# Last stage of a transformer layer on one Trainium2 core: the token sums move from VectorE to TensorE, the residual's shift to ScalarE, the scaled add to VectorE

## What is computed

```
x = x + layernorm(attention(layernorm(x)))
x = x + layernorm(ffn(layernorm(x)))
ffn(x) = y + z
y: mixture of 16 experts (128 -> 176 -> 128), each token goes to its best 2, weighted
z: shared expert (128 -> 352 -> 128)
layernorm(v) = (v - mean(v)) / sqrt(var(v) + 1e-5), over the 128 channels
```

## Time and profile before

| | before |
|---|---|
| median of 3 runs | 1185.89 us (1185.29 to 1187.51) |
| profiled execution: its own time | 1186.67 us |
| profiled execution: span of its profile | 1184.1 us |
| TensorE busy | 1055.4 us, 89% of the span |
| VectorE (DVE) busy | 845.6 us, 71% |
| ScalarE (ACT) busy | 738.9 us, 62% |
| GpSimd (POOL) busy | 846.1 us, 71% |

### The profile page before, as it was taken

One profiled execution on the slowest core, in us unless ns is written; L12 is line 12 of the kernel. 1 busy time (PEld: TensorE's weight loads), 2 busy tenths in 40 slices (PEclk: granted clock), 3 DMA queues, 4 the chain that ended last, 5 costly groups with the idle time before them and its releaser, 6 DMA issues.

```text
span 1184.1 us, 26787 instructions
## 1 busy us (share of the span) xinstructions
PE 1055.4 (89%) x8458; PEld 687.7 (58%) x8458; DVE 845.6 (71%) x2285; ACT 738.9 (62%) x1617; POOL 846.1 (71%) x984
## 2 busy tenths in 40 slices
PE   4589999999999999999999999999768999999700
PEld 2346555666656666566666665654336888888500
DVE  4587888778787787877878778774234666666586
ACT  1137778677776776867777677677524555555434
POOL 5455668878788788887888776566763666666567
PEclk8579999999999999999999999999969999999855
DMA  4341431433313233132431324224123445444275
GB/s 94 117 152 47 131 91 57 123 101 102 109 59 115 96 114 107 61 111 82 132 107 59 105 73 132 76 67 141 37 73 94 124 122 159 126 127 125 96 239 179
DMA packets 104854, 126.13 MB, mean 107 GB/s; under 512 B 17613, under 2 KB 85518, under 8 KB 100110
## 3 DMA queue, kind: packets, MB, share of 16 engines
q1 hardware_dynamic: 95624, 106.24, 30.7%
q0 software_dynamic: 8704, 18.11, 4.3%
q10 hardware_dynamic: 390, 0.10, 0.0%
HBM read 78.06 MB, written 45.42 MB: 104 GB/s over the span
## 4 chain that ended last, share of the span: by engine, by line
PE 84%; DVE 8%; POOL 2%; issue 2%; DMA 2%; ACT 1%; SPq 1%; POOLq 0%; DVEq 0%; ACTq 0%
PE heads_ps L1480 14%; PE score L1470 12%; PE wide L1508 12%; PE wide L1623 7%; PE wide L1446 6%; PE wide L1510 5%; PE score L1458 4%; PE wide L1604 3%; PE wide L1605 3%; PE score L1595 3%; PE misc L1488 2%; PE wide L1541 2%; PE wide L1621 2%; PE wide L1548 1%; DVE mx L1280 1%
## 5 line engine op out<-in xcount | busy, mean ns | idle before, releaser
L944 ACT ACTIVATE values<-score 128x512 f32<-128x512 f32 (+1 forms) x704 | 371.3, 558 | 122.4 <-PE score L1470 112.2
L1280 DVE TENSOR_REDUCE mx<-wide 128x2 f32<-128x1024 f32 (+3 forms) x384 | 392.9, 1042 | 72.7 <-PE wide L1510 68.2
L1508 PE MATMUL wide<-qk 72*128 72x512 bf16 (+3 forms) x1024 | 246.4, 305 | 7.7 <-DVE mx L1280 4.5
L853 POOL TENSOR_SCALAR_AFFINE_SELECT values<-values 128x512 f32<-128x512 f32 x256 | 173.8, 688 | 108.6 <-ACT values L944 107.3
L1470 PE MATMUL score<-qk 75*128 75x512 bf16 (+3 forms) x1024 | 229.5, 301 | 1.6 <-ACT values L944 0.9
L898 POOL DMA_INDIRECT token_scratch<-spread,e_id x144 | 137.9, 957 | 92.0 <-issue 74.5
L1510 PE MATMUL wide<-maskneg,identb 128*128 128x128 bf16 x1024 | 198.4, 222 | 0.0
L1480 PE MATMUL heads_ps<-values 128*32 128x512 f32 (+3 forms) x2048 | 175.3, 443 | 0.0
L842 POOL DMA_INDIRECT sorted_scratch<-zr,places x128 | 127.1, 993 | 30.7 <-issue 28.4
L1508 PEld LDWEIGHTS wide<-qk 72*128 72x128 bf16 x1024 | 101.0, 99 | 79.1 <-issue 17.2
L1470 PEld LDWEIGHTS score<-qk 75*128 75x128 bf16 x1024 | 87.3, 98 | 97.6 <-ACT values L944 46.9
(11 more groups left out here) (194 smaller groups left out, 1959.6 us busy)
## 6 DMA issues: line engine op xcount, KB each, us to landing
qk<-parts_scratch SPq DMA_DIRECT2D x192, 192.0 KB
parts_scratch<-spread SPq DMA_DIRECT2D x16, 768.0 KB
qk<-sorted_scratch SPq DMA_DIRECT2D x144, 66.0 KB
front<-token_scratch SPq DMA_DIRECT2D x16, 512.0 KB, 3.8
xt<-attn_x SPq DMA_DIRECT2D x16, 256.0 KB, 8.4
xr<-attn_x SPq DMA_DIRECT2D x16, 256.0 KB, 8.9
x_scratch<-z SPq DMA_DIRECT2D x16, 256.0 KB, 6.3
shared_scratch<-s_out SPq DMA_DIRECT2D x16, 256.0 KB, 8.5
```

Source lines behind the costliest of these rows:

```text
L853: nc.gpsimd.affine_select(out=prob[n][:, :, 0:P], in_=prob[n][:, :, 0:P], compare_op=ALU.is_ge, fill=0.0, base=0, pattern=[[0, HG], [1, P] ...
L944: nc.scalar.activation(free_ap(prob[kb][:, hs_[0], :], [[1, N * len(hs_)]]), score[SCORE_RING.buffer(b, step)][:, 0:N * len(hs_)], ACT.Exp ...
L1280: nc.vector.tensor_reduce(mx[:, h0:h0 + len(hs_), j:j + 1], src, axis=AX.X, op=ALU.max).then_inc(p1_max, 1)
L1508: nc.tensor.matmul(o, q4[e][0:ROWS, h, j * P:(j + 1) * P], k4[e][0:ROWS, h, 0:L], start=True, stop=False)
```

## The change

The sums go to TensorE: three accumulating f32 matmuls with the identity add the shared output and both expert outputs into one of four PSUM banks, ahead of which 40 filling matmuls are issued when the last expert output is ready. VectorE takes the statistics from PSUM. ScalarE no longer scales: it adds the shift to the layer's input, in place. VectorE multiplies the sum by the root, adds ScalarE's result and counts `c_ready` once per tile; in its order this finish stands two rows behind the statistics. POOL only takes roots. The small tiles get three copies in place of two, and SP issues the store of a row three rows later in its order.

```diff
+TAIL_FILL = 40
...
-C_STEPS = LN_STEPS + 1
+C_STEPS = LN_STEPS
...
+        NY, LAG, NC = 4, 3, 3
         (c_rstd, c_nmr, c_vareps, c_mv: NC copies instead of 2)
...
+        def c_sum(b):
+            return wide[b % 4 // 2][:, b % 2, :].rearrange("p (t c) -> p t c", t=NT)
...
@@ sync
             def tokens_in(b):
                 if b >= NY:
-                    sp.wait_ge(c_added, b - NY + 1)
+                    sp.wait_ge(c_summed, b - NY + 1)
                 sp.dma_start(c_y[b % NY].rearrange("p t k c -> p (t k c)"), token_v[b]).then_inc(c_in[b % NY], 16)
...
+            def tokens_out(b):
+                sp.wait_ge(c_ready, NT * (b + 1))
+                sp.dma_start(out_v[b], z_all[:, b, :, :]).then_inc(c_stored, 16)
+
             for b in range(B):
                 if b + NY < B:
                     tokens_in(b + NY)
-                sp.wait_ge(c_ready, b + 1)
-                sp.dma_start(out_v[b], z_all[:, b, :, :]).then_inc(c_stored, 16)
+                if b >= LAG:
+                    tokens_out(b - LAG)
+            for b in range(B - LAG, B):
+                tokens_out(b)
@@ gpsimd
             def root(b):
                 pool.wait_ge(c_varied, b + 1)
-                if b >= 2:
-                    pool.wait_ge(c_normal, NT * (b - 1))
-                nc.gpsimd.tensor_tensor(c_rstd[b % 2][:], c_vareps[b % 2][:], mhalf[:], ALU.pow).then_inc(c_rooted, 1)
-
-            def finish(b):
-                pool.wait_ge(c_normal, NT * (b + 1))
-                nc.gpsimd.tensor_tensor(z_all[:, b, :, :], z_all[:, b, :, :], x1_all[:, b, :, :], ALU.add).then_inc(c_ready, 1)
-
-            pool.wait_ge(x1_in, 16 * B)
+                if b >= NC:
+                    pool.wait_ge(c_ready, NT * (b - NC + 1))
+                nc.gpsimd.tensor_tensor(c_rstd[b % NC][:], c_vareps[b % NC][:], mhalf[:], ALU.pow).then_inc(c_rooted, 1)
+
             for b in range(B):
                 root(b)
-                if b >= 1:
-                    finish(b - 1)
-            finish(B - 1)
@@ scalar
+            act.wait_ge(x1_in, 16 * B)
             for b in range(B):
                 act.wait_ge(c_shift, b + 1)
                 for t in range(NT):
-                    nc.scalar.activation(z_all[:, b, t, :], z_all[:, b, t, :], ACT.Identity, bias=c_nmr[b % 2][:, t:t + 1],
-                                         scale=c_rstd[b % 2][:, t:t + 1]).then_inc(c_normal, 1)
+                    nc.scalar.activation(x1_all[:, b, t, :], x1_all[:, b, t, :], ACT.Identity,
+                                         bias=c_nmr[b % NC][:, t:t + 1]).then_inc(c_moved, 1)
@@ vector
-            def combine(b):
+            def measured(b):
                 cs.round(b)
-                dve.wait_ge(c_in[b % NY], 16 * (b // NY + 1))
-                if b == 0:
-                    dve.wait_ge(z_in, 16 * B)
-                z_b, y_b = z_all[:, b, :, :], c_y[b % NY]
-                cs.did(nc.vector.tensor_tensor(z_b, z_b, y_b[:, :, 0, :], ALU.add))
-                dve.wait_ge(c_step, cs.value())
-                nc.vector.tensor_tensor(z_b, z_b, y_b[:, :, 1, :], ALU.add).then_inc(c_added, 1)
-                dve.wait_ge(c_added, b + 1)
-                statistics(cs, z_b, f_st, c_mv[b % 2])
+                dve.wait_ge(c_summed, b + 1)
+                statistics(cs, c_sum(b), f_st, c_mv[b % NC])
...
             def shift(b):
                 dve.wait_ge(c_rooted, b + 1)
-                if b >= 2:
-                    dve.wait_ge(c_normal, NT * (b - 1))
+                if b >= NC:
+                    dve.wait_ge(c_moved, NT * (b - NC + 1))
...
+            def finish(b):
+                dve.wait_ge(c_moved, NT * (b + 1))
+                for t in range(NT):
+                    nc.vector.scalar_tensor_tensor(out=z_all[:, b, t, :], in0=c_sum(b)[:, t, :], scalar=c_rstd[b % NC][:, t:t + 1],
+                                                   in1=x1_all[:, b, t, :], op0=ALU.mult, op1=ALU.add).then_inc(c_ready, 1)
 
             for b in range(B):
-                combine(b)
+                measured(b)
                 if b >= 1:
                     shift(b - 1)
+                if b >= 2:
+                    finish(b - 2)
             shift(B - 1)
+            finish(B - 2)
+            finish(B - 1)
@@ tensor
+            def tokens_summed(b):
+                if b >= 4:
+                    pe.wait_ge(c_ready, NT * (b - 3))
+                pe.wait_ge(c_in[b % NY], 16 * (b // NY + 1))
+                if b == 0:
+                    pe.wait_ge(z_in, 16 * B)
+                nc.tensor.matmul(c_sum(b), ident[:], z_all[:, b, :, :], start=True, stop=False)
+                nc.tensor.matmul(c_sum(b), ident[:], c_y[b % NY][:, :, 0, :], start=False, stop=False)
+                nc.tensor.matmul(c_sum(b), ident[:], c_y[b % NY][:, :, 1, :], start=False, stop=True).then_inc(c_summed, 1)
+
+            pe.wait_ge(e_ready, NBLK)
+            kept_busy(TAIL_FILL)
+            for b in range(B):
+                tokens_summed(b)
```

More of the change, by code:

```diff
@@ L475, in program @@
         e_aT = [sb(f"e_aT{n}", [3 * P // 4, 2, P]) for n in range(2)]
-        NY = 4
+        NY, LAG, NC = 4, 3, 3
         c_y = [view(front, F32, [NT, TOPK, P], n * NT * TOPK * P) for n in range(NY)]
-        c_rstd = [sb(f"c_rstd{n}", [P, NT]) for n in range(2)]
-        c_nmr = [sb(f"c_nmr{n}", [P, NT]) for n in range(2)]
-        c_vareps = [sb(f"c_vareps{n}", [P, NT]) for n in range(2)]
-        c_mv = [sb(f"c_mv{n}", [P, NT, 2]) for n in range(2)]
+        c_rstd = [sb(f"c_rstd{n}", [P, NT]) for n in range(NC)]
+        c_nmr = [sb(f"c_nmr{n}", [P, NT]) for n in range(NC)]
+        c_vareps = [sb(f"c_vareps{n}", [P, NT]) for n in range(NC)]
+        c_mv = [sb(f"c_mv{n}", [P, NT, 2]) for n in range(NC)]
         f_rstd = sb("f_rstd", [P, NT])
@@ L556, in program @@
         c_step = sem("c_step")
-        c_added = sem("c_added")
+        c_summed = sem("c_summed")
         c_varied = sem("c_varied")
@@ L560, in program @@
         c_shift = sem("c_shift")
-        c_normal = sem("c_normal")
+        c_moved = sem("c_moved")
         c_ready = sem("c_ready")
@@ L1353, in _ @@
             cs = Steps(c_step, C_STEPS)
-            def combine(b):
+            def measured(b):
                 cs.round(b)
-                dve.wait_ge(c_in[b % NY], 16 * (b // NY + 1))
-                if b == 0:
-                    dve.wait_ge(z_in, 16 * B)
-                z_b, y_b = z_all[:, b, :, :], c_y[b % NY]
-                cs.did(nc.vector.tensor_tensor(z_b, z_b, y_b[:, :, 0, :], ALU.add))
-                dve.wait_ge(c_step, cs.value())
-                nc.vector.tensor_tensor(z_b, z_b, y_b[:, :, 1, :], ALU.add).then_inc(c_added, 1)
-                dve.wait_ge(c_added, b + 1)
-                statistics(cs, z_b, f_st, c_mv[b % 2])
+                dve.wait_ge(c_summed, b + 1)
+                statistics(cs, c_sum(b), f_st, c_mv[b % NC])
                 dve.wait_ge(c_step, cs.value())
                 cs.closed()
-                nc.vector.tensor_scalar(c_vareps[b % 2][:], c_mv[b % 2][:].rearrange("p t s -> p (t s)")[:, 1:2 * NT:2], EPS, None,
+                nc.vector.tensor_scalar(c_vareps[b % NC][:], c_mv[b % NC][:].rearrange("p t s -> p (t s)")[:, 1:2 * NT:2], EPS, None,
                                         ALU.add).then_inc(c_varied, 1)
@@ L1372, in shift @@
                 dve.wait_ge(c_rooted, b + 1)
-                if b >= 2:
-                    dve.wait_ge(c_normal, NT * (b - 1))
-                nc.vector.scalar_tensor_tensor(out=c_nmr[b % 2][:], in0=c_mv[b % 2][:].rearrange("p t s -> p (t s)")[:, 0:2 * NT:2],
-                                               scalar=-1.0, in1=c_rstd[b % 2][:], op0=ALU.mult, op1=ALU.mult).then_inc(c_shift, 1)
+                if b >= NC:
+                    dve.wait_ge(c_moved, NT * (b - NC + 1))
+                nc.vector.scalar_tensor_tensor(out=c_nmr[b % NC][:], in0=c_mv[b % NC][:].rearrange("p t s -> p (t s)")[:, 0:2 * NT:2],
+                                               scalar=-1.0, in1=c_rstd[b % NC][:], op0=ALU.mult, op1=ALU.mult).then_inc(c_shift, 1)
+            def finish(b):
[3 more added lines that the diff above has]
+                                                   in1=x1_all[:, b, t, :], op0=ALU.mult, op1=ALU.add).then_inc(c_ready, 1)
             for b in range(B):
-                combine(b)
+                measured(b)
                 if b >= 1:
                     shift(b - 1)
+                if b >= 2:
+                    finish(b - 2)
             shift(B - 1)
+            finish(B - 2)
+            finish(B - 1)
         @block.tensor
```

## The result

| | before | after |
|---|---|---|
| median of five runs | 1186.5 us (1185.29 to 1187.51) | 1181.14 us (1178.96 to 1182.95) |
| ratio, 95% interval | | 0.9958 (0.9946 to 0.9969) |
| profiled execution: own time, span | 1186.67, 1184.1 us | 1181.14, 1179.0 us |
| last expert output done to end of span ("the tail") | 66.34 us | 61.38 us |
| last work of any engine to end of span ("the end") | 3.55 us | 2.63 us |

The change is worth 5.0 us (3.7 to 6.4 by the interval) where 2.6 were forecast. The median lies inside the range on record, 0.24 us above its lower edge (1180.9). Of all executions in this document one is slow (3786.41 us, with the finish on POOL) and is left out of the ratios; the median of that kernel is 1181.22 us with it and 1181.04 without.

The account below looks back on a forecast made before the run. VectorE bound the last stage at 3.11 us per row; the four-bank loop would set 2.88. With 4.2 us won over 15 rows, 1.4 lost at the start and an even drain, 2.6 less: 1183.3 us, range 1180.9 to 1187.4.

Parts of the forecast that it names:

- TensorE's sum: Three f32 matmuls of 512 columns per batch row in the last stage: 6 x 0.43 = 2.58 us at full clock.
- The bank loop: Sums wait for VectorE's finish four rows back: two periods = 2.83 + 2.93 = 5.76 us, so 2.88 us per row.
- First statistics: VectorE's start on the first row, once its sum is complete: 1129.2 us, where before it was 1127.8.
- The turn: VectorE's work per row in the last stage: 1.67 + 1.08 = 2.75 us, between 2.51 and 3.07.
- The drain: From the last row's statistics at 1171.7 us through variance, root, shift, ScalarE and finish to 1178.0 us; about even with before.
- The end: After the last finish, the last store and the program's end: 3.55 us, as before the change.
- A cheap finish: Rival: VectorE's four finishing operations take 0.21 us each; 4.5 us less, 1181.4 us. Chance 0.17.
- No overlap: Rival: VectorE's finishing operations take 0.35 us each, VectorE needs 3.07 us per row and is the bound; 1186.1 us. Chance 0.12.
- A fixed latency for PSUM reads: Rival: VectorE's eight operations per row each take some 65 ns more from PSUM; 3.4 us more, 1189.3 us. Chance 0.05.
- The clock: Rival: TensorE's clock falls to half in the last stage, a sum takes 5.2 us; stage 35 us longer, 1221. Chance 0.04.
- Dearer passes: Rival: TensorE's passes take 0.50 us each beside the DMA engines' SBUF writes; stage 1.4 us longer, 1187.3 us. Chance 0.06.
- Loads that can't follow: Rival: DMA engines can't pass 85% busy, the period stays 3.11 us, time within 1.5 us of before. Chance 0.03.

Follow-up runs that it names:

- the interleaved kernel: Against the kernel with six banks and the shared output summed first: VectorE's finish of an earlier row put between statistics and aggregation; 1172.0 us, ratio 0.988.
- the late memset: The changed kernel plus one tiny POOL memset of 4 columns that waits for the last row's finish; 1181.18 us, one execution.

## Why the prediction was right

**The mechanism held, step by step.** TensorE's sum is 2.58 us per row (measured in the interleaved kernel as the pace itself). The bank loop is 5.68 us per two rows where 5.76 stood. First statistics came at 1129.15 where 1129.2 stood, a finishing operation every 0.26 us where 0.27 stood, and its duration is 343 ns where 0.35 us stood. The clock was 1.00 to the end of the sums. One sign on record looked different: the waits were to come in every row, 2.88 us apart and some 0.1 us each, and they came in every second row, 2.66 and 3.02 us apart with 0.28 us. The sum of two rows is what the loop fixes, and that came out. That it is a loop through banks, and not an engine that is full, was shown by changing the number of banks alone: tails of 119.64, 61.38 and 59.06 us with three, four and six.

**The sizes that were off** all lie on the same side, and add up to the missing 2.5 us (1179.0 for 1181.5):

| step of the forecast | on record | measured | earlier by |
|---|---|---|---|
| first statistics | 1129.2 us | 1129.15 us | 0.05 |
| first to last statistics | 42.5 us | 41.86 us | 0.64 |
| last statistics to the end of the last finish | 6.3 us | 5.36 us | 0.94 |
| the store and the end | 3.55 us | 2.63 us | 0.92 |

- *The turn.* It is 2.66 us and not 2.75. The four finishes hold VectorE for 1148.29 - 1147.26 = 1.03 us and not 1.08. And from the start of the epsilon operation to the shift it is 1147.18 - 1147.08 = 0.10 us now where it was 1141.62 - 1141.46 = 0.16 before: the operation itself took 0.25 us before and takes 0.17 now. In before it ended with POOL's add of that row, at 1141.71 and 1141.68 us:

```profile
1140.42 1.26 POOL L912 TENSOR_TENSOR qk<-qk,values 128x512 f32<-128x512 f32 x1 [0.28 <-ACT qk L1049]
...
1141.62 0.15 DVE L1375 SCALAR_TENSOR_TENSOR c_nmr<-c_mv,c_rstd 128x4 f32<-128x4 f32 x1
```

  This is the hold that the kernel with the finish on POOL shows at full size. In the kernel with the adds on VectorE and no add on POOL the operation takes 0.17 us. So the turn too got cheaper through a neighbour that the change removed.
- *The drain.* I put the root at 1.34 us, between its two prices beside VectorE and alone, without asking which of VectorE's operations makes it dear. It is VectorE's adds (1.41 and 1.45 us beside them in the kernel that keeps them), and the change removes them: 1.01 us. And I carried ScalarE's 1.65 us for four operations over as "the same count and shape", though the new form reads one small tile where the old read two: 1.28 us. These are 0.33 and 0.37 of the 0.94; the largest of the rest is 0.09, from the last statistics to the root (1.69 us where 1.78 stood).
- *The end.* I carried 3.55 us over although the change takes POOL away from the end of the work. Nothing in the trace of before could have priced this. It could have been named as a term that only one row supports, with an engine under it that the change moves. The trace of after and the late memset put it at 0.9 to 1.1 us.

One reading of before on record is a little off, without effect on the time: its 15 rows were not all 3.11 us apart. The first two steps were 2.95 and 3.03, so first to last statistics took 46.42 us, and 3.9 us were to be won there, not 4.2.

**The rivals.** A cheap finish: refuted, 0.26 us from start to start and not 0.21; its time of 1181.4 us came out nearly, but for other reasons, which is a warning against judging a theory by the total. No overlap: refuted by the same 0.26. A fixed latency for PSUM reads: refuted, 283 ns out of PSUM against 280 out of SBUF for the same statistics, and 343 against 345 for the finish (the second in the kernel with the adds on VectorE); the Trainium skill's rule (VectorE: DVE Perf Modes, the section on the TRN2 errata) adds 62 cycles, an estimated 65 ns, and does not hold here. The clock: not in after, but one bank fewer brought it about. Dearer passes: refuted, sums at 2.58 us in the interleaved kernel with the DMA share at 1.02. Loads that can't follow: refuted by 316 and 347 GB/s where the change draws at most 267 over ten microseconds of its loop.

**The chances.** Faster by over 0.2% had 0.50, and it is what came. Since 2.6 us of gain lay just past a bound of 2.4, errors of a few tenths in a handful of terms decided the sign of the statement. That it went the right way, and that 1181.14 fell inside a range from 1180.9, is in part luck: the gain came out nearly twice the forecast, and only about half of it was in the sum. The carried-over terms were taken at their old price. Here the neighbours that the change removed had made them dearer, so the sum leaned to one side.

## What to carry to other kernels

Before counting on a new producer and consumer pair, write the ring as an equation: with N banks and a finish L rows behind, N - L periods hold one consumer turn and one producer sum, and the period is that or the slowest engine's own time, whichever is longer (3 banks: 5.66 us per row while the clock was full; 4 banks: 2.84; 6 banks: the consumer's own 2.65). Where the producer has to be kept busy ahead of the data, look first for the part of its real work whose inputs are already there; it was worth 2.5 us here over plain filling. And when a step leaves an engine, price again what ran beside it and what ends the program, not only the step.

## What the runs showed that was not expected

- **VectorE and POOL hold each other up inside instructions.** POOL's root on 128x4 elements takes 1.01 us alone or beside VectorE's finish out of PSUM, 1.13 beside the finish out of SBUF, 1.46 beside VectorE's adds of two SBUF tiles. In the other direction a VectorE operation on 128x4 elements went from 0.17 to 1.30 us beside POOL's 1.26 us add and ended with it, and from 0.17 to 0.25 in the kernel before. This is busy time in every view; it shows only when the same instruction is compared between two stretches or two kernels.
- **The last engine matters.** From the last work to the end of the span it was 2.63 to 2.71 us in the kernels where VectorE worked last, and 3.55, 3.56 and 3.61 in those where POOL did. The third is the only run made to test it.
- **ScalarE's price goes with its small operands.** 390 ns for 128x128 with a bias tile, in after and in the kernel with the adds on VectorE; 481 with a bias and a scale tile; 457 with both and the data from PSUM. No run changes the small operands alone.
- **A clock at half speed came back under the work itself** in the kernel without filling: 0.50, then 0.70 on average over 1125 to 1127 us, then 1.00, with TensorE idle for 8.84 us ahead of 1123.39 us and busy without a break behind it. In the kernel with three banks, where it rests in each row, it averaged 0.73 over 60 us.
